# The first loads, the last row tile of layer 1's attention, its thought loop and its gated output of a four-layer Flamingo kernel, put in another order

## The chip, the cores and the metric

The kernel runs on one core of a Trainium2 chip. The metric is the device time of one execution in microseconds (us). The kernel before has 3995.62 us, the median of three runs (3991.7, 3995.62 and 3998.26).

## The reference

A batch of 4 sequences of 512 rows with 512 columns passes four layers. Each layer adds a cross-attention and a feed-forward part, both on layer-normed rows, each scaled by the tanh of a gate:

```
x = x + tanh(g_xattn[i]) * xattn_i(ctx, layernorm(x))      # i = 0, 1, 2, 3
x = x + tanh(g_ffn[i])   * ffn_i(layernorm(x))
```

- Layer 0's attention builds a graph from the context: similarities of projected queries and keys, sigmoid, and of each row only the 153 largest entries are kept. Its feed-forward part is a SwiGLU of width 2048; in this kernel its down weights first pass a Hadamard transform of length 2048.
- Layer 1's attention forms scores of 512 columns for each row, layer-norms them with a gamma and a beta, takes the softmax and adds it to x.
- Layer 1's feed-forward part takes the last row of each sequence, norms it, multiplies it by `agg_w` and repeats four times `thought = thought + (gelu(norm(thought) * pn_gamma + pn_beta) @ d1_w + d1_b) @ d2_w + d2_b` (the gelu is of the product with `d1_w`). Then `broadcast = thought @ bc_w + bc_b`, `gate = sigmoid(x @ gate_w + gate_b)`, and the output is `layernorm(x + gate * broadcast) * out_gamma + out_beta`.
- Layer 2's attention has 32 query heads of 16 columns over 8 key heads. Its feed-forward part is a mixture of 8 experts, top 2.
- Layer 3 is an attention with folded weights and rope, and a SwiGLU.

All data are float32.

## The kernel before

All of x lies in SBUF as `X`, 16 tiles of 128 rows; a batch has four. Each engine has its own program, and the programs are joined by semaphores. A big area `AR` is used by every stage in turn. PSUM has four pairs of banks (BM, BR, BS, BT), each pair a ring.

**The start.** SyncE (SP) issues the loads one after another (L2605 to L2614): the first batch of x, the whole context `CT`, the identity, the gates, gamma; then the query and key weights, the Hadamard matrix and the 4 MB of down weights; then the rest of x, and four writes of zeros to a routing table in DRAM (L2617). PE, ACT and DVE all wait for the first five. DVE norms batch 0 and adds its share of it (`add_norm`). PE and ACT make the similarities. Then DVE and ACT find the 153rd largest entry of each row by a search in 32 steps: in each step both count how many entries lie above a trial value (L728 on DVE, L639 on ACT), and DVE sets the next trial. Beside it POOL does four stages of butterflies of the Hadamard transform, two instructions of 128x4096 each (L307). After the search DVE keeps the top entries (`keep_top`, L766 to L775), PE turns the graph (`turn_graph`), then PE multiplies 16 tiles by the 128x128 Hadamard matrix (L581), and ACT takes each from PSUM (L665). Then comes the transpose of the normed batch (L233), and the loop of layer 0's feed-forward part, in which the other three searches and three of the four batches of layer 1's attention are placed beside the products.

**Layer 1's attention, last batch.** After that loop DVE norms batch 3, PE turns it and makes scores for four row tiles (L572), ACT copies them (L652). DVE takes the moments of all four tiles (`l1_moments`), POOL the reciprocal root, DVE norms them, multiplies by gamma, adds beta (L821), takes the maximum, ACT the exponentials (L657), and DVE adds them to x (`l1_add`). Then SP copies the last row of the batch to a tile of four rows, `XL`, and `l1f_vector` begins.

**The thought loop.** DVE norms `XL` twice; PE multiplies it by `agg_w` (L994); DVE adds a bias (L1184) and norms it (`norm_thought`: moments L1150 to L1152, root on POOL, L1154, times gamma L1155, plus beta L1156, all on 4 rows of 512). Each of four steps: PE turns the four rows (L987), DVE copies them (L1189), PE multiplies by `d1_w` (L1047), DVE adds a bias (L1198), ACT takes the gelu, PE turns and multiplies by `d2_w` (L1064) and sums four parts (L1068), DVE adds a bias (L1212) and the old thought (L1213), and norms. Where DVE waits for PE it does pieces of the norms of x that the gates need (`x_moments`, `x_rows`) and adds beta to x (`add_beta`, L1181). PE does one of batch 0's four gate products per step (L1012). The last `norm_thought` result isn't used.

**The gated output.** PE makes small products of the thought (L1002). Then for batch 1, 2 and 3: two gate products, the transposes of the previous batch's mixed rows (`turn_mixed`, L1020), two gate products, and the norm's transposes of the next batch (L233), which for the last of the three is batch 0, for layer 2's queries. ACT takes the sigmoids (L1091), the copies (L1096) and the norm's scaling (`scale_rows`, L1101); DVE mixes (`mix_gate`, L1227), takes moments (`out_moments`, L1234), and adds to x (`add_mixed`, L1246 and L1248). The order is written out by hand in each engine's program. DVE cuts the queries in two parts (L1269), SP stores them (L1488) and loads them spread out over heads (L1473).

**Layer 2.** PE, ACT, DVE and POOL all wait until x is done for layer 1 (`x_done` of 4 * B); SP waits for its third batch. PE makes the scores of the first two head groups (L1546), DVE their maxima (L1726), POOL cuts the maxima in two parts (`cut_max`), PE turns them (L1555), ACT copies them, SP puts them into the query tile, and the loop of layer 2 begins. In it, batch by batch, the routing of tokens to experts is worked out, and POOL scatters each token's number to its slot in the table, 128 numbers of 4 bytes per DMA, 8 DMAs per batch (`scatter_tokens`, L1409). For the last batch this is done in `moe_pool`; when all have landed, POOL gathers rows of the table (L2135), PE turns them, and the expert loop starts.

Of the kernel before, what the change touches and what calls it, by code (L numbers as in the profile page):

```python
# [13 lines left out]
P = 128  # L14
# [12 lines left out]
TW = NT + 2  # L27
EK = 3
# [62 lines left out]
def flamingo(nc, x, ctx_n, ctx_t, gates, gamma_raw, ident, l0_wq, l0_wk, hadamard, l0_w13, l0_w2, l1_wk, l1_bk, l1_bk_row,  # L91
# [3 lines left out]
    with ctx:  # L95
# [159 lines left out]
        WH = [a(HID // P, D), a(HID // P, D)]  # L255
        TRIAL_I, DROP_I, DROP_P = TRIAL.bitcast(I32), DROP.bitcast(I32), BS[:, 0, 0:ST].bitcast(I32)
# [11 lines left out]
        COLS = a(2 * KT)  # L268
        OROWS = a(2, D)
        BCT, T0 = a(4 * B), a(4 * B)  # L270
        assert a.here() <= FFN_AREA, a.here()
# [13 lines left out]
        def keys_pool(pool):  # L285

            pool.wait_ge(l0f.m.full, 2 + ST + HAD_M)
            nc.gpsimd.tensor_copy(KXH.bitcast(F32R), CT).then_inc(kx_hi, 1)
# [6 lines left out]
        def had_pool(pool):  # L295

            pool.wait_ge(l0_had, 32)
            n = 0
            for stage in range(4):
                w = 1 << stage  # L300
                of, to = WH[stage % 2], WH[1 - stage % 2]
# [140 lines left out]
        HAD_M = HID // P  # L442
        NU = B * ST * UG
# [3 lines left out]
        FFN0_DONE = 3 * B - 1  # L447

# [50 lines left out]
        def l0_tensor(pe):  # L499
# [69 lines left out]
            def l1_scores():  # L569
                pe.wait_ge(f.m.free, m.now() + 2)  # L570
                for st in range(ST):
# [3 lines left out]
            pe.wait_ge(l0_w, 32)  # L575
# [7 lines left out]
            norm_tensor(pe)  # L583
            pe.wait_ge(turn.free, T_PE.now() + 2)
            for b in range(B):
                for g in range(ST):
# [16 lines left out]
                    if g == 2 and b:  # L603
                        l1_scores()
# [11 lines left out]
            l1_scores()  # L616

        def l0_scalar(act):
# [8 lines left out]
            def similarities(b):  # L627
                act.wait_ge(graph_ready, b * ST + 1)
# [20 lines left out]
            def l1_scores(b):  # L649
                act.wait_ge(prob1_used, b + 1)  # L650
                for st in range(ST):
                    nc.scalar.copy(PROB1[:, st, :], full(act, f.m, m)).then_inc(f.m.free, 1)  # L652

            def l1_exp(b):
                act.wait_ge(norm1_ready, b + 1)
                for st in range(ST):
                    nc.scalar.activation(PROB1[:, st, :], PROB1[:, st, :], ACT.Exp, bias=NEGM1[:, st:st + 1],  # L657
                                         accum_out=SUM1[:, st:st + 1]).then_inc(exp1_done, 1)

            project()  # L660
            similarities(0)
            count(BITS)
            tr.step()
            for t in range(HAD_M):
                nc.scalar.activation(WH[1][:, t, :], full(act, f.m, m), ACT.Copy, scale=float(HID ** -0.5)).then_inc(f.m.free, 1)  # L665
# [37 lines left out]
            l1_exp(B - 1)  # L703

        def l0_vector(v):
# [9 lines left out]
            scale1 = float(512 ** -0.5)  # L715
# [86 lines left out]
            def l1_moments():  # L802
# [8 lines left out]
                nc.vector.tensor_scalar(VAR1, MV[:, :, 1], scale1 * scale1, EPS_INNER, ALU.mult, ALU.add).then_inc(var1_ready, 1)  # L811

            def l1_normed(b):
                v.wait_ge(root1_ready, b + 1)
                link(v, nc.vector.tensor_scalar(RS1, RS1, scale1, None, ALU.mult))
# [35 lines left out]
            v.wait_ge(x_rest, 16)  # L851
# [56 lines left out]
            l1_moments()  # L908
            l1_normed(B - 1)
            l1_max()  # L910
            l1_add(B - 1)

        def l0_pool(pool):

            def root1(b):
                pool.wait_ge(var1_ready, b + 1)
                nc.gpsimd.tensor_tensor(RS1, VAR1, HALF[:, :], ALU.pow).then_inc(root1_ready, 1)

# [12 lines left out]
            root1(B - 1)  # L931
# [4 lines left out]
        COL["bc"], COL["gate"] = COLS[:, 0:KT], COLS[:, KT:2 * KT]  # L936
        a = area(FFN_AREA)
        GT, OT, ON = a(KT, S), a(KT, S), a(ST, D)
# [5 lines left out]
        TB = a(4, D)  # L944
# [1833 lines left out]
```

## Time and profile before

| | |
|---|---|
| median of three runs | 3995.62 us |
| the profiled execution | 4001.03 us |
| its span, first to last instruction | 3999.2 us |
| PE busy | 3661.6 us (92%) |
| DVE busy | 1982.6 us (50%) |
| ACT busy | 1377.6 us (34%) |
| POOL busy | 355.7 us (9%) |
| mean share of DMA engines on the main hardware queue | 21.0% |

The busy row of PE in 40 slices of 100 us is 9 or more nearly everywhere. It is 1 in the first slice (0 to 100 us), 8, 6, 7 and 8 between 800 and 1200 us, and 5 from 1600 to 1700 us. So one looks at these places, and there the waits of PE and the chain of waits tell what PE waits for.

### The profile page before, as it was taken

The page shows a single profiled execution, that of the slowest core. Times are in us where ns is not written, and L with a number is a line of the kernel's source. Part 1 is how long each engine was busy: PE and PEld are TensorE (multiplying, and loading weights), DVE is VectorE, ACT ScalarE, POOL GpSimd, SP SyncE. Part 2 cuts the span into 40 slices and gives each one's busy share as a digit, 9 for nine tenths or more (in the row PEclk, how much of TensorE's full clock was granted, in tenths as well). Part 3 has the DMA queues.
Part 4 walks back from the last instruction along what each step waited for, and adds up shares of the span by engine and source line. Part 5 has one row for each costly group of instructions (what it writes and reads, how often), then busy time and mean ns, then how long its engine had stood idle before and what let it go on. Part 6 is the DMA issues. An engine that isn't in the chain of part 4 may idle for free.

```text
span 3999.2 us, 35714 instructions
## 1 busy us (share of the span) xinstructions
PE 3661.6 (92%) x11789; PEld 1695.6 (42%) x11790; DVE 1982.6 (50%) x3587; ACT 1377.6 (34%) x2838; POOL 355.7 (9%) x380
## 2 busy tenths in 40 slices
PE   1999999986789999599879999999999999999999
PEld 0444444432445444356534444444444434444443
DVE  8556666145678776211156756656565652111111
ACT  5524242011357667122233443434343441100100
POOL 7000000000123231211111100000000000000000
PEclk6999999998889999799989999999999999999999
DMA  3321312300322322455532101010101102222221
GB/s 119 126 79 54 132 57 75 112 23 22 86 69 62 74 59 82 156 162 160 170 133 67 50 32 36 24 36 24 36 24 36 36 1 84 85 78 79 84 84 52
DMA packets 78347, 295.90 MB, mean 74 GB/s; under 512 B 10856, under 2 KB 11752, under 8 KB 66684
## 3 DMA queue, kind: packets, MB, share of 16 engines
q1 hardware_dynamic: 69856, 268.35, 21.0%
q0 software_dynamic: 8352, 25.78, 2.1%
q8 instruction: 77, 1.26, 0.1%
q14 instruction: 62, 0.51, 0.0%
HBM read 255.73 MB, written 33.64 MB: 72 GB/s over the span
## 4 chain that ended last, share of the span: by engine, by line
PE 79%; DVE 8%; issue 7%; ACT 3%; DMA 2%; POOL 1%; SPq 0%; DVEq 0%; POOLq 0%; ACTq 0%
PE BM L2293 6%; PE BM L2348 5%; PE BM L529 5%; PE BR L529 5%; PE BR L2357 4%; PE BM L364 4%; PE BR L364 4%; PE BS L2331 3%; PE BS L545 3%; PE BT L545 3%; PE BT L2340 3%; PE BM L2306 3%; PE BR L1989 3%; PE BM L1978 2%; PE BR L1978 2%
## 5 line engine op out<-in xcount | busy, mean ns | idle before, releaser
L2422 ACT ACTIVATE AR<-BS,AR 128x512 f32<-128x512 f32 x256 | 174.5, 685 | 411.5 <-DVE AR L2517 411.5
L2416 ACT COPY AR<-BM 128x512 f32<-128x512 f32 x340 | 198.8, 585 | 307.2 <-PE BM L2348 99.9
L2530 DVE SCALAR_TENSOR_TENSOR X<-BR,AR,X 128x512 f32<-128x512 f32 x256 | 191.9, 750 | 206.2 <-PE BR L2357 197.1
L2517 DVE TENSOR_REDUCE AR<-BS 128x2 f32<-128x1024 f32 x128 | 156.9, 1226 | 253.8 <-PE BS L2331 253.8
L2357 PE MATMUL BR<-AR 128*128 128x512 f32 x512 | 254.8, 621 | 4.2 <-DVE X L2530 0.6
L2348 PE MATMUL BM<-AR 128*128 128x512 f32 x512 | 246.7, 594 | 0.0
L2293 PE MATMUL BM<-XT,AR 128*128 128x512 f32 x512 | 236.6, 605 | 0.7 <-ACT XT L239 0.7
L364 PE MATMUL BM<-XT,AR 128*128 (+1 forms) x512 | 231.7, 595 | 4.9 <-DMA AR<-l_w_dram 4.9
L419 DVE TENSOR_TENSOR AR<-AR,BR 128x512 f32<-128x512 f32 x64 | 44.0, 688 | 379.5 <-PE BR L364 379.5
L529 PE MATMUL BM<-XT,AR 128*128 128x512 f32 x512 | 230.6, 593 | 0.9 <-ACT AR L632 0.9
L529 PE MATMUL BR<-XT,AR 128*128 128x512 f32 x512 | 230.2, 592 | 0.0
L364 PE MATMUL BR<-XT,AR 128*128 (+1 forms) x512 | 230.2, 592 | 0.0
L1664 ACT ACTIVATE PT<-BS 128x512 f32<-128x512 f32 x340 | 192.4, 596 | 86.1 <-PE BS L1562 81.4
L639 ACT ACTIVATE AR<-AR 128x512 f32<-128x512 f32 x256 | 182.6, 714 | 88.8 <-DVE AR L751 88.6
L728 DVE TENSOR_SCALAR_CACHE_REDUCE AR<-AR 128x512 f32<-128x512 f32 x264 | 186.3, 743 | 3.5
L2340 PEld LDWEIGHTS BT<-ID,AR 128*128 128x128 f32 x1024 | 128.6, 142 | 136.8 <-issue 125.3
L1726 DVE TENSOR_REDUCE NEG<-BM 128x2 f32<-128x1024 f32 x129 | 157.6, 1221 | 53.5 <-PE BM L1546 52.0
L2428 ACT COPY AR<-BT 128x512 f32<-128x512 f32 x256 | 151.5, 592 | 75.0 <-PE BT L2340 74.8
L1726 DVE TENSOR_REDUCE NEG<-BR 128x2 f32<-128x1024 f32 x127 | 155.0, 1221 | 41.1 <-PE BR L1546 38.0
L226 POOL TENSOR_TENSOR RSTD<-VAR,HALF 128x4 f32<-128x4 f32 x32 | 32.6, 1020 | 1550.9 <-DVE VAR L2546 930.3
L399 ACT ACTIVATE AR<-BM 128x512 f32<-128x512 f32 x64 | 38.3, 598 | 362.3 <-PE BM L364 362.1
L1562 PE MATMUL BS<-QS,KS 128*128 128x512 f32 x340 | 149.2, 441 | 14.7 <-DMA QS<-MTS 12.3
(383 smaller groups left out, 5919.0 us busy)
## 6 DMA issues: line engine op xcount, KB each, us to landing
AR<-l_w_dram SPq DMA_DIRECT2D x128, 512.0 KB, 3.5
AR<-l_wq_dram SPq DMA_DIRECT2D x32, 1152.0 KB, 5.2
AR<-l_w_dram SPq DMA_DIRECT2D x42, 768.0 KB, 4.9
AR<-w2h SPq DMA_DIRECT2D x16, 1024.0 KB, 4.8
QS<-qx SPq DMA_DIRECT2D x32, 512.0 KB, 10.0
AR<-l_w_dram SPq DMA_DIRECT2D x16, 1024.0 KB, 4.8
AR<-l_w_dram SPq DMA_DIRECT2D x8, 1408.0 KB
made<-AR SPq DMA_DIRECT2D x40, 256.0 KB, 4.9
```

The source lines that it names most:

```text
L364: last = nc.tensor.matmul(bank.rearrange("p (a n) -> p a n", a=1), w[:, kt, a, :], XT[:, ds(b & 1, 1), kt, :], start=kt == 0, stop=kt == K ...
L529: last = nc.tensor.matmul(bank, w[:, kt, a, :], XT[:, b & 1, kt, :], start=kt == 0, stop=kt == KT - 1)
L545: last = nc.tensor.matmul(S_BANKS[st], f.HIDDEN[:, u, st * P:(st + 1) * P], f.DOWN[:, u, :], start=u == 0, stop=u == UG - 1)
L728: nc.vector.tensor_scalar(DUMP[:, st, :], SIM[:, st, :], bound, None, ALU.is_ge, ALU.add, accum_out=COUNTED[:, st:st + 1]).then_inc(found, 1)
L1664: nc.scalar.activation(PT2[:, tt, h, :], evict(("e", n, tt, h)), ACT.Exp, scale=float(HD ** -0.5)).then_inc(e_free, 1)
L1726: nc.vector.tensor_reduce(NEG2[:, n % 2, u // 2, to:to + 2], unit(("s", n, u))[:, 0:2, :], op=ALU.max, axis=AX.X, negate=True).then_inc(s_ ...
L2293: last = nc.tensor.matmul(bank, WS[:, p % 2, at:at + P], XT[:, b % 2, kt, :], start=kt == 0, stop=kt == KT - 1)
L2340: last = nc.tensor.transpose(BT[:, L3[job] % 2, st * P:(st + 1) * P], PROB3[h][:, st, lt * P:(lt + 1) * P], ID[:, :])
L2348: last = nc.tensor.matmul(BM[:, L3[job] % 2, :], KVN[:, p // 8 * ST + lt, :], PROBT3[:, lt, :], start=lt == 0, stop=lt == ST - 1)
L2357: nc.tensor.matmul(BR[:, L3[job] % 2, :], CC3[h][:, st * P:(st + 1) * P], W3[:, p % 8 * 2 + h, :], start=True, stop=True)\
L2416: nc.scalar.copy(to, BM[:, L3[job] % 2, :]).then_inc(m_free, 1)
L2530: nc.vector.scalar_tensor_tensor(out=xb, in0=BR[:, L3[job] % 2, :], scalar=RS3[:, p % 2, h, st:st + 1], in1=xb, op0=ALU.mult, op1=ALU.add) ...
```

## The change

Parts, in the order of the program:

1. First loads: batch 0's quarter of the context, the two weights and the Hadamard matrix come first; PE starts on these four; x, identity and gates follow, then the down weights, the rest of the context and of x. ACT makes its tanh and sigmoid of the gates after its first copies, and takes batch 0's similarities without waiting for DVE.
2. POOL does three stages of butterflies, from the end of `add_norm` on; the fourth is done by PE, which sums two products per tile. Ten of the 16 tiles are put ahead of the graph's turning, and ACT takes five of them between the last five steps of the search.
3. The table in DRAM is 16 times as wide: each 4-byte slot has 64 bytes for itself. It is zeroed by one DMA of 1 MB in 128-byte pieces; a gathered row has 8 KB for 512 bytes.
4. Layer 1's last batch: the fourth row tile, which holds the last row, is scored, normed and added first. The three others are normed by DVE while PE multiplies by `agg_w`, exponentiated by ACT, and added in the first thought step.
5. Thought's gamma and beta are applied to the turned tile (128 rows of 16), `d2`'s bias is added to the thought beside the `d1_w` product, and the unused last norm is left out. The pieces of the norms of x move by one place.
6. The gated output: one gate product ahead of `turn_mixed(0)`, the norm's transposes directly behind `turn_mixed`, and for the last batch ahead of it, so that the queries are cut and stored earlier; `scale_rows` comes before the last sigmoid; DVE's order changes with it. The memsets of layer 2's tiles are done at the end of the thought loop, and SP's copies of these wait only for batch 0's mixing. The last batch is scaled and added to x by POOL.
7. Layer 2's PE, its first maxima on DVE, and the SP no longer wait for the whole of x; ACT's exponentials and DVE's loop do.

```diff
@@ Hadamard on POOL and PE
-            pool.wait_ge(l0_had, 32)
+            pool.wait_ge(l0_had, 16)
+            pool.wait_ge(vec, ADD_NORM)
-            for stage in range(4):
+            for stage in range(HAD_STAGES):          # HAD_STAGES = 3
...
+            def last_butterfly(t):
+                bank, half = start_job(pe, f.m, m), HAD_M // 2
+                nc.tensor.matmul(bank, HAD, WH[0][:, t % half, :], start=True, stop=False)
+                nc.tensor.matmul(bank, HAD if t < half else NHAD, WH[0][:, t % half + half, :], start=False, stop=True)\
+                  .then_inc(f.m.full, 1)
+            pe.wait_ge(l0_w, 64)
             project(0)
             similarities()
+            pe.wait_ge(butterflies, 2 * HAD_STAGES)
+            for t in range(HAD_EARLY):               # 10
+                last_butterfly(t)
+            pe.wait_ge(loaded, 64)
             turn_graph(0)
-            pe.wait_ge(butterflies, 8)
-            for t in range(HAD_M):
-                nc.tensor.matmul(start_job(pe, f.m, m), HAD, WH[0][:, t, :], start=True, stop=True).then_inc(f.m.full, 1)
+            for t in range(HAD_EARLY, HAD_M):
+                last_butterfly(t)
@@ ACT
-            count(BITS)
+            count(BITS - HAD_BETWEEN)                # HAD_BETWEEN = 5
+            for t in range(HAD_BETWEEN):
+                take_hadamard(t)
+                count(1)
@@ layer 1's last batch on DVE
-            l1_moments()
-            l1_normed(B - 1)
-            l1_max()
-            l1_add(B - 1)
+            l1_last_rows()
+            def l1_last_rows():
+                v.wait_ge(f.m.free, m.step() + 2)
+                stats_tiles1(v, ST - 1, ST)
+                v.wait_ge(root1_ready, B)
+                link(v, nc.vector.tensor_scalar(RS1[:, ST - 1:ST], RS1[:, ST - 1:ST], SCALE1, None, ALU.mult))
+                norm_tiles1(v, ST - 1, ST)
+                v.wait_ge(f.m.free, m.step(3) + 2)
+                stats_tiles1(v, 0, ST - 1)
+                add_tiles1(v, B - 1, ST - 1, ST, (B - 1) * ST + 1)
@@ thought
-                link(v, nc.vector.tensor_scalar(TR[0:B, :], TH[0:B, :], ML[0:B, 0:1], RL[0:B, :], ALU.subtract, ALU.mult))
-                link(v, nc.vector.tensor_tensor(TR[0:B, :], TR[0:B, :], TB["pn_g"], ALU.mult))
-                nc.vector.tensor_tensor(TR[0:B, :], TR[0:B, :], TB["pn_b"], ALU.add).then_inc(th_ready, 1)
+                nc.vector.tensor_scalar(TR[0:B, :], TH[0:B, :], ML[0:B, 0:1], RL[0:B, :], ALU.subtract, ALU.mult).then_inc(th_ready, 1)
+            def take_turned():
+                link(v, nc.vector.tensor_tensor(turned, cols(full(v, lr, r)[:, 0:4 * B]), over_b(COL["pn_g"], KT), ALU.mult))
+                nc.vector.tensor_tensor(turned, turned, over_b(COL["pn_b"], KT), ALU.add).then_inc(lr.free, 1)
+            v.wait_ge(root1_ready, B + 1)
+            norm_tiles1(v, 0, ST - 1)                # beside the agg product
...
-                nc.vector.tensor_copy(turned, cols(full(v, lr, r)[:, 0:4 * B])).then_inc(lr.free, 1)
+                take_turned()
+                link(v, nc.vector.tensor_tensor(TH[0:B, :], TH[0:B, :], TB["d2"], ALU.add))
                 if k == 0:
-                    x_moments(1)
+                    add_tiles1(v, B - 1, 0, ST - 1, B * ST)
...
-                link(v, nc.vector.tensor_tensor(TR[0:B, :], bank[0:B, :], TB["d2"], ALU.add))
-                nc.vector.tensor_tensor(TH[0:B, :], TH[0:B, :], TR[0:B, :], ALU.add).then_inc(lr.free, 1)
+                nc.vector.tensor_tensor(TH[0:B, :], TH[0:B, :], bank[0:B, :], ALU.add).then_inc(lr.free, 1)
-                norm_thought()
+                if k < K_STEPS - 1:
+                    norm_thought()
@@ gates on PE                                     # GATES_FIRST = {1: 1, 2: 2, 3: 2}
             for b in range(1, B):
-                for mt in range(2):
+                for mt in range(GATES_FIRST[b]):
                     gate(b, mt)
+                if b == B - 1:
+                    norm_tensor(pe)
                 turn_mixed(b - 1)
-                for mt in range(2, KT):
+                if b < B - 1:
+                    norm_tensor(pe)
+                for mt in range(GATES_FIRST[b], KT):
                     gate(b, mt)
-                norm_tensor(pe)
@@ gates on DVE
             mix_gate(0)
+            x_moments(3)
             out_moments(0)
+            x_rows(3)
             mix_gate(1)
             add_mixed(0)
-            x_moments(3)
-            x_rows(3)
+            x_moments(0)
             add_beta(3)
             out_moments(1)
+            x_rows(0)
             mix_gate(2)
             add_mixed(1)
-            x_moments(0)
-            x_rows(0)
+            cut_first_queries()
             out_moments(2)
             mix_gate(3)
...
             add_mixed(2)
             out_moments(3)
-            add_mixed(3)
@@ POOL, the last batch
+            pool.wait_ge(on_ready, ST * B)
+            xb = X[:, (B - 1) * ST:B * ST, :]
+            nc.gpsimd.tensor_tensor(ON, ON, OROWS[:, 0:1, :].to_broadcast([P, ST, D]), ALU.mult).then_inc(out_norm, 1)
+            pool.wait_ge(out_norm, B + 1)
+            nc.gpsimd.tensor_tensor(xb, xb, ON, ALU.add).then_inc(x_done, 1)
@@ layer 2
-            pe.wait_ge(x_done, 4 * B)                # PE; DVE and ACT: moved behind the first maxima
-            sp.wait_ge(x_done, 3 * B + 1)
+            sp.wait_ge(mix_done, KT + 1)             # ahead of the copies QS, KS
-                sp.wait_ge(x_done, 4 * B)
+                sp.wait_ge(negm_ready, B)            # ahead of the values
@@ the table                                       # APART = 16
-        table = nc.dram_tensor("table", [P * P, 1], F32, kind="Internal").ap()
+        table = nc.dram_tensor("table", [P * P * APART, 1], F32, kind="Internal").ap()
@@ first loads on SP
+            sp.dma_start(CT[:, 0:S], ctx_t[:, 0:S]).then_inc(l0_w, 16)
+            sp.dma_start(WQ0, l0_wq).then_inc(l0_w, 16)
+            sp.dma_start(WK0, l0_wk).then_inc(l0_w, 16)
+            sp.dma_start(HAD, hadamard).then_inc(l0_w, 16)
             sp.dma_start(X[:, 0:ST, :], x_tiles[:, 0:ST, :]).then_inc(loaded, 16)
-            sp.dma_start(CT, ctx_t).then_inc(loaded, 16)
...
+            sp.dma_start(WH[1], l0_w2).then_inc(l0_had, 16)
+            sp.dma_start(CT[:, S:], ctx_t[:, S:]).then_inc(x_rest, 16)
             sp.dma_start(X[:, ST:, :], x_tiles[:, ST:, :]).then_inc(x_rest, 16)
-            for c in range(4):
-                sp.dma_start(table.rearrange("(p n) o -> p (n o)", p=P)[:, 32 * c:32 * c + 32], ZERO[:, :]).then_inc(table_zero, 16)
+            sp.dma_start(table.rearrange("(p a n) o -> p a (n o)", p=P, n=32),
+                         ZERO[:, :].rearrange("p (o n) -> p o n", o=1).to_broadcast([P, P * APART // 32, 32])).then_inc(table_zero, 16)
```

## Rows read from the trace of the kernel before

**Rows 1.** The page, busy us of each engine (share of the span) and instructions.
```profile
PE 3661.6 (92%) x11789; PEld 1695.6 (42%) x11790; DVE 1982.6 (50%) x3587; ACT 1377.6 (34%) x2838; POOL 355.7 (9%) x380
```

**Rows 2.** Timeline, 0 to 120 us: start, duration, engine, line, [idle before, releaser].
```profile
10.55 2.47 DVE L210 BATCH_NORM_STATS2 STAT<-X 128x6 f32<-128x512 f32 x4 [10.55 <-DMA GC<-gamma_raw_dram]
...
17.50 0.60 ACT L631 ACTIVATE AR<-BM 128x512 f32<-128x512 f32 x1 [2.27 <-DVEq L711]
...
20.68 70.95 POOL L307 TENSOR_TENSOR AR<-AR 128x4096 f32<-128x4096 f32 x8 [5.72 <-DMA AR<-l_w_dram]
...
22.79 0.06 DVE L733 MEMSET AR<- 128x4 f32 x1 [2.31 <-ACT AR L632]
...
85.24 6.41 DVE L766 SCALAR_TENSOR_TENSOR AR<-AR 128x2 f32<-128x2 f32 x1
...
96.59 1.97 PE L520 MATMUL BS<-ID,AR 128*128 128x128 f32 x8 [75.12 <-DVE AR L775]
...
100.06 15.66 PE L581 MATMUL BM<-AR 128*128 128x512 f32 x32
...
115.56 1.04 PE L233 MATMUL BT<-ID,XN 128*128 128x128 f32 x8
...
117.77 4.51 POOL L290 TENSOR_TENSOR AR<-AR 128x2048 fp32r<-128x2048 f32 x1
```

**Rows 3.** Windows: stretch, length, busy by engine (instructions), granted clock, DMA share, GB/s.
```profile
100.00:102.00 2.00, 2.00 (x5) 0.97 (x4) 2.00 (x4) 0.00 (x0) 0.00 (x0) 0.50 0.00 0
102.00:104.00 2.00, 2.00 (x5) 0.77 (x5) 1.74 (x4) 1.27 (x3) 0.00 (x0) 0.94 0.00 0
```

**Rows 4.** DMA issues by line: KB each, median us from issue to landing.
```profile
X<-x_dram SPq DMA_DIRECT2D x1, 3072.0 KB, 23.1
...
table<-ZERO SPq DMA_DIRECT2D x4, 16.0 KB, 8.6
...
CN<-ctx_n_dram SPq DMA_DIRECT2D x1, 0.5 KB, 13.3
```

**Rows 5.** Timeline, 887 to 923 us: last batch of attention, start of thought.
```profile
887.91 1.50 DVE L805 BATCH_NORM_STATS2 STAT<-AR 128x6 f32<-128x512 f32 x2 [12.85 <-ACT AR L652]
...
895.27 4.62 DVE L821 TENSOR_TENSOR AR<-AR 128x2048 f32<-128x2048 f32 x2
...
910.27 0.17 DVE L1138 MEMSET AR<- 128x128 f32 x1 [0.66 <-DMA AR<-X]
...
922.99 0.68 DVE L1184 TENSOR_TENSOR AR<-BR,AR 4x512 f32<-4x512 f32 x1 [6.75 <-PE BR L994]
```

**Rows 6.** Groups of DVE, 909 to 1010 us: count, busy us, mean ns.
```profile
L1155 DVE TENSOR_TENSOR AR<-AR 4x512 f32<-4x512 f32 x5 | 3.4, 681 | 0.2
```

**Rows 7.** Timeline, 1003 to 1127 us: end of thought, gates, start of layer 2.
```profile
1003.33 3.70 PE L1012 MATMUL BM<-XT,AR 128*128 128x512 f32 x8
...
1008.90 0.38 PE L987 MATMUL BR<-ID,AR 4*128 4x4 f32 x4 [1.87 <-DVE AR L1156]
...
1064.56 1.04 PE L1020 MATMUL BS<-ID,AR 128*128 128x128 f32 x8
...
1080.13 1.04 PE L233 MATMUL BT<-ID,XN 128*128 128x128 f32 x8
...
1106.49 1.19 PE L1546 MATMUL BM<-KS,QS 128*128 128x512 f32 x2 [11.39 <-DVEq L1715]
...
1120.83 1.57 POOL L1815 TENSOR_SCALAR VW<-CN,G 128x512 f32<-128x512 f32 x1 [13.03 <-DMA AR<-moe_token_dram]
...
1126.53 1.05 PE L1555 MATMUL BS<-ID,NM 128*8 128x128 f32 x4
```

**Rows 8.** Chain of waits, 1600 to 1665 us: start, us, what.
```profile
1637.01 12.43 DMA table<-AR
...
1654.73 3.31 DMA AR<-xnd,AR
```
**Rows 9.** Window of 2 us in that wait, columns as in rows 3.
```profile
1642.00:1644.00 2.00, 0.00 (x0) 0.00 (x0) 0.00 (x0) 0.00 (x0) 0.00 (x0) 0.50 0.00 0
```

More of the change, by code:

```diff
@@ L27 @@
 TW = NT + 2
+APART = 16
 EK = 3
@@ L447, in flamingo @@
         FFN0_DONE = 3 * B - 1
+        SCALE1 = float(512 ** -0.5)
+        TILES1 = {b: (0, 1, 2, 3) if b < B - 1 else (3, 0, 1, 2) for b in range(B)}
         def l0_table():
@@ L615, in l0_tensor, with exp_tiles1, norm_tiles1, add_tiles1 @@
             l1_context()
-            l1_scores()
+            l1_scores(B - 1)
+        def exp_tiles1(act, lo, hi, ready):
+            act.wait_ge(norm1_ready, ready)
+            for st in range(lo, hi):
+                nc.scalar.activation(PROB1[:, st, :], PROB1[:, st, :], ACT.Exp, bias=NEGM1[:, st:st + 1],
+                                     accum_out=SUM1[:, st:st + 1]).then_inc(exp1_done, 1)
+        def norm_tiles1(v, lo, hi):
+            tiles = PROB1[:, lo:hi, :]
+            for st in range(lo, hi):
+                last = nc.vector.tensor_scalar(PROB1[:, st, :], PROB1[:, st, :], MV[:, st, 0:1], RS1[:, st:st + 1], ALU.subtract, ALU.mult)
+            link(v, last)
+            for row, op in ((0, ALU.mult), (1, ALU.add)):
+                link(v, nc.vector.tensor_tensor(tiles, tiles, ROWS1[:, row:row + 1, :].to_broadcast([P, hi - lo, S]), op))
+            nc.vector.tensor_reduce(NEGM1[:, lo:hi], tiles, op=ALU.max, axis=AX.X, negate=True).then_inc(norm1_ready, 1)
+        def add_tiles1(v, b, lo, hi, done):
+            v.wait_ge(exp1_done, done)
+            link(v, nc.vector.reciprocal(SUM1[:, lo:hi], SUM1[:, lo:hi]))
+            link(v, nc.vector.tensor_scalar(SUM1[:, lo:hi], SUM1[:, lo:hi], G[:, 1:2], None, ALU.mult))
+            for st in range(lo, hi):
+                last = nc.vector.scalar_tensor_tensor(out=X[:, b * ST + st, :], in0=PROB1[:, st, :], scalar=SUM1[:, st:st + 1],
+                                                      in1=X[:, b * ST + st, :], op0=ALU.mult, op1=ALU.add)
+            last.then_inc(prob1_used, 1)
+        def stats_tiles1(v, lo, hi):
+            for st in range(lo, hi):
+                last = nc.vector.bn_stats(STAT[:, st, :], PROB1[:, st, :])
+            link(v, last)
+            for st in range(lo, hi):
+                last = nc.vector.bn_aggr(MV[:, st, :], STAT[:, st, :])
+            link(v, last)
+            nc.vector.tensor_scalar(VAR1[:, lo:hi], MV[:, lo:hi, 1], SCALE1 * SCALE1, EPS_INNER, ALU.mult, ALU.add).then_inc(var1_ready, 1)
         def l0_scalar(act):
@@ L1116, in l1f_scalar @@
                 act.wait_ge(mix_done, b * KT + 1 if b > 1 else 1)
[L1117 removed]
+                for mt in range(GATES_FIRST[b]):
                     sigmoid(GT, mt)
+                if b == B - 1:
+                    for kt in range(KT):
+                        nc.scalar.copy(QHL[:, 0, kt, :], full(act, turn, T_ACT)).then_inc(q_hi, 1)
                 take_mixed(b - 1)
[L1120 to L1121 removed]
                 if b < B - 1:
                     norm_scalar(act, (b + 1) & 1)
[L1124 to L1127 removed]
+                for mt in range(GATES_FIRST[b], KT):
+                    sigmoid(GT, mt)
+                    if mt == KT - 2:
+                        scale_rows(b - 1)
             take_mixed(B - 1)
```

162 lines of the change are left out of this document (85 added, 77 removed).

## The prediction, made before the changed kernel was run

> **What bounds the kernel now.** I read the page first: PE is busy 92% of the span [rows 1], and the slices in the section on the profile leave three places where it isn't: the first 120 us, 850 to 1130 us, and 1600 to 1700 us. Outside them the change touches nothing, so each microsecond won or lost in one of the three moves everything behind it. Then the timelines of the three.
>
> In the first, the search runs from 22.79 to 85.24: 32 steps in 62.45, 1.95 each. POOL's butterflies run from 20.68 for 70.95, 8.87 each, and end at 91.6; DVE's first small operation after the search takes 6.41 and ends there too, since it waits for POOL. PE turns the graph from 96.59, does the Hadamard tiles from 100.06, and reaches the norm's transposes only when these are over, at 115.56 [rows 2]. In the second there is one chain from DVE to PE and back; PE waits for it. In the third PE waits for a transfer: the last scatter to the table lands 12.43 after its issue begins [rows 8], though in the wait no engine works and the DMA engines move nothing [rows 9].
>
> **Prologue.** Loads: the first five carry 2.1 MB and free DVE at 10.55 [rows 2]. At about 400 GB/s (2.1 MB in the 5 us before), now 1.5 MB lie ahead: about 8.0, so -2.5. ACT's similarities no longer wait for DVE's end (2.27 at 17.50 [rows 2]); they follow PE, whose project starts some 5 us earlier. Both branches, DVE's 7 us of norm and 2.7 of add_norm and ACT's four pairs, meet at about 18. The search starts at 18.2, not 22.79: -4.6.
>
> POOL now starts when add_norm ends, 18.2 too (the down weights land at about 18), and does 6 instructions: 18.2 + 6 x 8.87 = 71.4. ACT has done 27 steps at 18.2 + 27 x 1.95 = 70.9 and then waits for the first Hadamard tile. A tile is now two products, four matmul pieces. At the half clock a piece takes 0.86 (15.66 / 32 is 0.49 over both levels); the clock stood at 0.50 until 102 and at 0.94 behind [rows 3], 5.5 us after PE began to work at 96.59 [rows 2]. So tile 0 is full at 71.4 + 3.5 = 74.9, ACT goes on at 75.5 and tile 1 is late by about 1.4 too; from then on a tile takes 4 x 0.43 = 1.72 and hides in the step, which grows by 0.2 (0.6 of copy against 0.4 of idle time). The search ends at about 87.5, 2.3 later than now. But the 6.41 is gone: keep_top takes 4.9 from there (91.7 to 96.6), so the graph is ready at 92.7, 3.9 earlier. PE is then still at tile 9; it turns the graph at 93 to 95.3 and has only 6 tiles left, 6 x 1.72 = 10.3: norm's transposes at 105.5, where DVE's norm is ready (two microseconds before). Against 115.56 that is **-10**. Bounds: if PE stays at the half clock, 16 tiles x 3.44 from 71.4 on put the transposes at about 128, +12; if the first tile didn't hold the search, -13. I take -10, since in rows 3 work of this kind raised the clock.
>
> The table's zeros: 8192 rows of 128 bytes on SP's queue, ahead of the first up weights. They start when the rest of x has landed, at about 29 (5.6 + 23.1 [rows 4]). From below: the four old writes, 128 such rows each, were issued 0.6 apart and the last three landed alike 8.6 behind their issue [rows 4], so at most 0.6 per 128 rows: 64 x 0.6 = 38. From above: the load of 2048 rows of 512 bytes landed in 13.3 [rows 4]: 4 x 13.3 = 53. The weights follow at 67 to 82 + 5, and are needed at 110. Cost 0; cover 23 us.
>
> **Last row tile.** Old axis: ACT's first score tile is there at 887.9, DVE's memset, which waits for the copied row, at 910.27 [rows 5]. New: moments of one tile 1.2, root 1.1, scaling 0.6, gamma and beta 2 x 0.69 and maximum 0.6 (a quarter of the tiles in 4.62 for two [rows 5], with fixed parts): 893.1. The exponential (0.9) hides behind the other three tiles' moments, 2.5. Then 1.2 for the add, 1.9 for the row's copy: 898.8, **-11.5**. The deferred scaling, gamma, beta and maximum of three tiles (1.5 + 2 x 1.73 + 1.7 = 7.0) lie beside the agg product; that chain takes 6.75 [rows 5], so DVE is 0.2 late: -11.3. Exponentials of three tiles (2.7) are over before the first step asks for them; their add (3.3) and the d2 bias (0.7) fit the 5.2 of the d1 product. The gate weights are loaded after this add; they land about 2.5 before the first gate product: a thin cover.
>
> **Thought.** Per norm, gamma and beta go: 2 x 0.68 and gaps = 1.43 [rows 6]; the turned tile gets a second small operation: +0.22. Four norms: -4.84. The bias in the four steps: -0.72 each (the same size of instruction), -2.88. At the fourth step's sum the gain is 11.3 + 3 x 0.72 + 4 x 1.21 = 18.3. The last norm is gone, but PE is in its gate product, 1003.33 + 3.70 = 1007.03 [rows 7]; it turned at 1008.90: 1.8 more. **-20.1** up to the broadcast.
>
> **Gates and layer 2.** Batch 1's PE work is the same in another order, and PE is its bound: 0. In batch 3 the queries' transposes ran at 1080.13; between the two first gate products, which ended at 1064.56, and these lay turn_mixed(2) with a wait for DVE, and two gate products [rows 7]. They now come first: at 1064.6. DVE has x ready (x_rows(0) at about 1056 on this axis) and cuts them by 1069, where the store began at 1085.8: queries are in SBUF by about 1084. Then PE: turn_mixed(2) 3.2, two gate products 6.9: 1077.5. ACT sigmoid, scale_rows, sigmoid: 1078.5. DVE: mixing 1079.3, add_mixed(2) 4.6 (the size of L821 [rows 5]): 1083.9, out_moments(3) 5.8: 1089.7. DVE's first maximum of layer 2 followed 1106.49 by 1.3; it is now at 1089.8: -18.0. Its 16 maxima, 1.14 each, set the pace as before, and PE's turn_max moves from 1126.53 [rows 7] to 1108.5. POOL is beside: ACT's scaling until 1092.7, two instructions of 128x2048 at 4.51 [rows 2]: x done at 101.9 past 1000, that is 6.6 before it is needed. The values, 14.5 after 1089.7, are there at 1104, maxima cut at 1106: 2.3 of cover (before, POOL waited 13.03 for them [rows 7], also hidden). **-18.0**. Bounds: if PE kept its full clock after the thought loop, about 4 more; if the cover of POOL or values is gone, or one wait per batch stays, 10 less.
>
> **Table.** Eight scatters of 128 numbers wrote into 64 KB; neighbours in an expert lie 4 bytes apart, so some 16 writes of a scatter fall into one 64 bytes. The row says that the time is spent behind the last moved byte [rows 8, 9]. If it is these writes waiting for each other, a slot of 64 bytes for each takes it away, and the scatter lands like the gather of rows of x, in 3.31 [rows 8]: -9.1. The gather of 1 MB for 64 KB adds 1 MB / 0.4 = +2.4. Together -6.7; bounds -8 and +2.4. I take -6.7, nearer to what the idle DMA engines suggest.
>
> The Trainium skill, page "DMA: Bandwidth & Descriptors", section "Specifications", says that transfers under 512 bytes are done by read-modify-write. By that rule a 4-byte write stays as dear in a wide table, and this part would be +2.4; the trace has no scatter with other spacing to decide it. This is the second rival.
>
> **Sum.** -10 - 20.1 - 18.0 - 6.7 = -54.8. The profiled execution took 4001.03; 4001 - 55 = 3946. It lies 5.4 above the median, so 3995.6 - 54.8 = 3941.
>
> **Rivals.**
> 1. The search is held more than I count, or the gates' new order leaves one wait per batch. For it: ACT has 0.4 idle per step only, and PE must warm up; both are places where I chained three engines. Prologue -4, gates -12: 3941 + 12 = 3953.
> 2. The wide table doesn't shorten the landing and costs its gather: 3941 + 9 = 3950. For it: the elements are still 4 bytes. Against: nothing moves in those 11 us.
> 3. Slower: the zeros. If a row of 128 bytes costs one of the 16 DMA engines more than (110 - 29 - 5) / 512 = 0.15, the first unit of layer 0 waits, and from 0.15 + 55 / 512 = 0.26 on all the gain is lost; at 0.3, 29 + 154 + 5 = 188 in place of 110: +78 - 55, 4018. Against it: 13.3 / 128 = 0.10 for rows of 512 bytes.
> 4. PE doesn't warm between the evictions: +22, 3963.
>
> **Chances.** The sum 0.5, rival 1 0.2, rival 2 0.2, rival 4 0.06, rival 3 0.03, a reordering that gains nothing 0.01. 0.2% is 8 us, what a measurement here tells from no change. Faster 0.95, same 0.02, slower 0.03. The range takes in the clock's 4, the search's 3 and the table's 1.3 below, and as much again for small gains left at 0, and rivals 1, 2 and 4 above: 3926 to 3963.
>
> **What would show it.** Search from about 18 to 87 with one gap of 4 to 5 in ACT at about 71 (Hadamard tile 0); DVE's operation behind the search at 0.2, not 6.4; first transposes at 105. The row's copy 11.5 earlier; thought's steps 18.5 apart, not 20.4; the queries' store 36 earlier in all behind the prologue; layer 2's turn_max 38 + 10 earlier; POOL's last scatter landing in about 4. Wrong would be: PE at 0.50 through the tiles, up weights landing after 105, DVE waiting in the first step for exponentials, PE waiting for the gate weights.

## The result, and the profile after

Before 3994.9 us, after 3922.7 us, medians of 4 runs each: ratio 0.982, 95% interval 0.9803 to 0.9837. The change takes 72.2 off; 54.8 was forecast, and 3922.7 lies 3.3 below the range's lower end. The profiled execution of after took 3922.4 with a span of 3920.6, that of before 4001.0 with 3999.2, so the two traces differ by 78.6. Some 6 of these are the high execution of before.

The page of after, busy us by engine, beside [rows 1]:

```profile
PE 3659.5 (93%) x11821; PEld 1693.0 (43%) x11822; DVE 1960.4 (50%) x3582; ACT 1376.8 (35%) x2839; POOL 348.5 (9%) x380
```

PE's busy time is 2 us shorter and the span 79: what went was waiting. The timeline of after, 0 to 120 us, against [rows 2]:

```profile
10.38 2.47 DVE L211 BATCH_NORM_STATS2 STAT<-X 128x6 f32<-128x512 f32 x4 [10.38 <-DMA GC<-gamma_raw_dram]
...
20.25 0.06 DVE L792 MEMSET AR<- 128x4 f32 x1
...
20.44 53.25 POOL L312 TENSOR_TENSOR AR<-AR 128x4096 f32<-128x4096 f32 x6 [5.67 <-DVE X L780]
...
73.74 2.07 PE L585 MATMUL BM<-AR 128*128 128x512 f32 x2 [58.23 <-POOL AR L312]
...
77.56 0.60 ACT L710 ACTIVATE AR<-BM 128x512 f32<-128x512 f32 x1 [5.14 <-PE BM L586]
...
79.59 0.16 DVE L803 TENSOR_SCALAR BS<-AR 128x2 int32<-128x2 f32 x1 [5.25 <-ACT AR L691]
...
88.04 0.16 DVE L825 SCALAR_TENSOR_TENSOR AR<-AR 128x2 f32<-128x2 f32 x1
...
93.32 1.04 PE L528 MATMUL BS<-ID,AR 128*128 128x128 f32 x8
...
105.47 1.09 PE L234 MATMUL BT<-ID,XN 128*128 128x128 f32 x8
```

The reader sees the forecast's picture: one gap of 5.14 in ACT, the 6.41 of DVE's small operation gone (0.16), the norm's transposes at 105.47 in place of 115.56. POOL starts when DVE's `add_norm` (L780) ends, at 20.44, and is done at 73.69.

Timeline, 876 to 902 us, against [rows 5]: one score tile goes ahead alone and frees the row's copy.

```profile
876.66 0.69 DVE L662 BATCH_NORM_STATS2 STAT<-AR 128x6 f32<-128x512 f32 x1 [10.71 <-ACT AR L704]
...
884.80 0.50 SPq L1042 DMA_DIRECT2D AR<-X  x1
...
886.60 0.17 DVE L1215 MEMSET AR<- 128x128 f32 x1 [1.17 <-DMA AR<-X]
...
899.46 0.67 DVE L1266 TENSOR_TENSOR AR<-BR,AR 4x512 f32<-4x512 f32 x1
```

Timeline, 951 to 1061 us, against [rows 7]: thought's last sum, the queries' transposes, the first product and maximum of layer 2, POOL's two instructions for the last gated batch.

```profile
969.64 0.68 DVE L1299 TENSOR_TENSOR AR<-AR,BR 4x512 f32<-4x512 f32 x1 [1.20 <-PE BR L1140]
...
973.16 0.41 PE L1060 MATMUL BR<-ID,AR 4*128 4x4 f32 x4
...
1024.67 1.04 PE L234 MATMUL BT<-ID,XN 128*128 128x128 f32 x8
...
1050.19 1.19 PE L1640 MATMUL BM<-KS,QS 128*128 128x512 f32 x2 [4.25 <-DMA QS<-qx]
...
1051.42 1.23 DVE L1820 TENSOR_REDUCE NEG<-BM 128x2 f32<-128x1024 f32 x1 [2.01 <-PE BM L1640]
...
1052.45 3.81 POOL L1396 TENSOR_TENSOR AR<-AR 128x2048 f32<-128x2048 f32 x1 [3.23 <-ACT AR L1176]
```

The chain of waits around the table, against [rows 8]. The scatter no longer stands in it as a transfer; the gather behind it, 1 MB now, holds its place:

```profile
1565.70 1.04 POOL table L1505
1566.74 1.20 issue
...
1568.70 0.99 POOL AR L2230
1569.69 5.65 issue
...
1575.57 3.18 DMA AR<-xnd,AR
```

And the part that the prediction did not have: layer 2's loop over heads. The waits of PE in it, summed (us in total, times, longest), first before, 1128 to 1613:

```profile
PE BS L1562 <- DMA QS<-MTS: 12.3, 3, 5.6
...
PE BT L1562 <- DMA QS<-MTS: 1.0, 1, 1.0
```

then after, 1071 to 1543:

```profile
PE BS L1656 <- DMA QS<-MTS: 3.3, 1, 3.3
```

MTS are the turned maxima, which SP writes as rows into the queries' tile, 8 KB at a time. The 3.3 that is left in after is also in before, as a wait of 3.37 at 1130.95, long before the first scatter of the loop (1346.59). The longest wait of before comes after POOL has issued four scatters, from 1346.59 to 1351.53. SP issues two rows between 1352.14 and 1353.33, and PE goes on with them only at 1363.32; the second line is the window of 13 us from the end of this wait, with the granted clock as the third number from the end (1.00 is full speed, 2.4 GHz; 0.50 is 1.2 GHz):

```profile
1363.32 0.80 PE L1562 MATMUL BS<-QS,KS 128*128 128x512 f32 x1 [5.63 <-DMA QS<-MTS]
```
```profile
1363.00:1376.00 13.00, 12.68 (x57) 6.62 (x58) 7.80 (x9) 7.31 (x14) 1.45 (x3) 0.78 0.02 3
```

In after the same two rows are issued between 1295.50 and 1296.69, PE's product at the same place starts at 1300.90 without a wait, and the clock is 1.00 in the 13 us from 1293 on and in the next:

```profile
1306.00:1319.00 13.00, 12.73 (x69) 6.76 (x72) 12.26 (x19) 9.51 (x18) 6.17 (x8) 1.00 0.56 126
```

From the first store of cut queries to the last store of normed rows this loop took 1085.8 to 1612.9 before (527.1) and 1029.5 to 1542.0 after (512.5).

Where the 78.6 of the traces come from, by equal points in both:

| stretch | forecast | traces |
|---|---|---|
| start to layer 1's last norm (861) | -10 | -9.1 |
| context products before the last scores | 0 | -2.1 |
| last row tile, up to thought's first norm | -11.3 | -12.3 |
| thought, up to the broadcast | -8.8 | -12.2 |
| gates, up to the first maximum | -18.0 | -20.7 |
| layer 2's loop | 0 | -14.5 |
| table and routing | -6.7 | -7.7 |
| sum | -54.8 | -78.6 |

### The profile page after: what moved, and what is told of

It is laid out like the page before. It is cut to its first block, busy times and chain, and to the rows that moved or that the text cites. A ratio compares the mean times of both kernels' runs of the same rounds, so it can differ in the third digit from the quotient of the medians.

```text
span 3920.6 us, 35772 instructions
## 1 busy us (share of the span) xinstructions
PE 3659.5 (93%) x11821; PEld 1693.0 (43%) x11822; DVE 1960.4 (50%) x3582; ACT 1376.8 (35%) x2839; POOL 348.5 (9%) x380
## 4 chain that ended last, share of the span: by engine, by line
PE 82%; DVE 7%; issue 6%; POOL 2%; DMA 2%; ACT 1%; SPq 0%; DVEq 0%; POOLq 0%; ACTq 0%
PE BM L2388 6%; PE BM L2443 5%; PE BM L537 5%; PE BR L537 5%; PE BR L2452 4%; PE BM L369 4%; PE BR L369 4%; PE BS L2426 4%; PE BS L553 3%; PE BT L553 3%; PE BT L2435 3%; PE BR L2084 3%; PE BM L2401 3%; PE BT L1666 3%; PE BM L2073 2%
## 5 line engine op out<-in xcount | busy, mean ns | idle before, releaser
L2452 PEld LDWEIGHTS BR<-AR 128*128 128x128 f32 x512 | 86.3, 189 | 171.1 <-DVE X L2625 89.0
```

Source lines behind the costliest of these rows:

```text
L2452: nc.tensor.matmul(BR[:, L3[job] % 2, :], CC3[h][:, st * P:(st + 1) * P], W3[:, p % 8 * 2 + h, :], start=True, stop=True)\
```

## The experiments

All times are medians; 3 rounds each, 5 in the last group. The kernel before stood at 3995.0, 3995.7, 3997.2 and 3994.8 beside the four groups.

**Slots 4 bytes apart in the changed kernel.**

```diff
-APART = 16
+APART = 1
...
-SHIFTED, idx, 15, None, ALU.arith_shift_right
+SHIFTED, idx, 11, None, ALU.arith_shift_right
```

> The changed kernel with table slots 4 bytes apart again, in 64 KB; all else is left as changed. Theory A (in layer 2's loop the rows of maxima, which PE waits for, are held up behind scatters that write neighbouring 4-byte slots): the loop from its first turned maxima to the store of the last normed batch takes 484 to 485 again in place of 470.3, PE waits some 9 us more for the maxima's transfers, and the last scatter lands 12 late: 3922.7 + 7.8 + 14.5 = 3945, 3940 to 3947. Theory B (the loop's 14.5 came from elsewhere: another alignment of the transfers or of the granted clock after earlier parts moved): only the table's own 7.8 comes back, 3930.5, and the loop stays at 470.

3940.8, 18.1 above the changed kernel. The loop takes 523.7 (1029.9 to 1553.6); counted as in the expectation, from the first rows of maxima, it is 481.7 against 470.2 in after, so 11.5 of the 14.5 are back. PE's waits in it and the landing of the last scatter are back too:

```profile
PE BS L1656 <- DMA QS<-MTS: 9.9, 3, 4.3
```
```profile
1577.28 12.15 DMA table<-AR
```

Theory A. Of the 18.1, 7.2 is the table's own chain (last store of rows to the first store of expert rows 58.6, against 51.4); the loop gives the rest, 11.2 in this trace.

**The wide table alone in the kernel before.** The edit is the table's part of the change, nothing else.

```diff
+APART = 16
...
-table = nc.dram_tensor("table", [P * P, 1], ...)
+table = nc.dram_tensor("table", [P * P * APART, 1], ...)
...
-nc.vector.tensor_copy(idx[...], POS)
+nc.vector.tensor_scalar(idx[...], POS, float(APART), None, ALU.mult)
```

> The kernel before with nothing but the wide table (64 bytes a slot) and its zeros, its number arithmetic and its gather. Theory A: 3994.9 - 7.8 - 14.5 = 3973, 3970 to 3976; the loop from its first turned maxima to the last normed batch's store takes 470 and not 484.7, and runs of it agree within 2 us where those of the kernel before spread over 6.6. Theory B (loop gained by alignment): 3987. The zeros cost nothing in either: first up weights still land before 110.

3979.1 (3974.7 to 3980.8), 15.8 below before. The loop takes 512.6 (1083.1 to 1595.7), 470.2 by the expectation's count and as expected; PE waits 3.3 for maxima in it; the last scatter lands in 2.20. The expected 3973 was taken from one high profile of before, and is 6 low; the runs spread as widely as before, so the stalls are not what spreads them. Theory A for the cause; its size in medians is 16 to 18, table and loop together, by this run and the one above.

**Narrow slots, all scatters behind the loop.** (`APART` is 1 and the shift 11 here too.)

```diff
 if routed_batch(n, 6) is not None:
-    scatter_tokens(pool, routed_batch(n, 6), 0)
+    pass
...
-for j in range(2):
-    scatter_tokens(pool, B - 1, j)
+for b in range(B):
+    for j in range(2):
+        scatter_tokens(pool, b, j)
```

> The changed kernel with slots 4 bytes apart and the scatters of batches 0 to 2 taken out of layer 2's loop and issued in front of the last batch's, after the loop. Theory A: without scatters in it the loop takes 470 although the table is narrow; behind it POOL issues 24 more scatters at 1.27 = 30.5 and the last lands 10 late or more: 3922.7 + 30.5 + 7.8 = 3961, up to 3980 if the scatters queue on each other. Theory B: the loop's time doesn't follow the scatters; the end is the same.

3959.5, next to the 3961 of theory A. With a narrow table and no scatter in it, the loop takes 511.9 (1029.5 to 1541.4), and PE waits 3.3 for maxima. Behind it 32 scatters queue on each other:

```profile
1579.60 33.11 DMA table<-AR
```

From the first issue at 1540.0 to this landing at 1612.7 it is 72.7 for 32, 2.27 each, against the 1.27 that POOL takes to issue one. So the stalls come with dense scatters inside the loop, and with nothing else that was varied. That a row of maxima lands late because it has to pass such scatters on its way is the reading that fits; the traces show PE's wait for the row and not what held the row up.

**How far apart is far enough.** Only APART and the shift differ from the changed kernel (`APART` 4 and a shift of 13, then 2 and 12).

> The changed kernel with slots 16 bytes apart in place of 64: the table is 256 KB, its zeros a quarter, its gather 256 KB and not 1 MB. Theory A1 (a write is held up only by neighbours in the same 64 bytes, so the cost grows with how many share one): four share one instead of sixteen, the last scatter lands in 2.3 + 10.2 x 3/15 = 4.3, gather 1.8 shorter, loop nearly free of stalls: 3923, 3920 to 3927. Theory A2 (any write closer than some larger distance is held up alike, as with a rule on transfers under 512 bytes): the landing stays at 12 and the loop at 484: 3943. Theory A3 (16 bytes already suffice): 3921.

> The changed kernel with slots 8 bytes apart, a table of 128 KB. Slots 16 and 64 bytes apart let the last scatter land in 2.2, 4 bytes apart in 12.15. If what counts is how many bytes of a small unit (16 or 8) two writes share: 8 bytes may be as free as 16, landing 2.2, gather 0.3 shorter than at 16: 3917.5. If the unit is 16 bytes: two slots share one, a landing of some 5 and stalls of 2 to 5 in layer 2's loop: 3922 to 3926.

> The changed kernel with slots 16 bytes apart once more, beside the changed kernel itself on the same chip: 3917.9 again, 4 to 5 below it; from the traces 2.3 of it is the shorter gather (3.35 in place of 5.65 behind its issue). If the rest was the granted clock of the prologue and not the table, it lies between 2.3 and 5 here.

> The changed kernel itself, as the other side of the comparison: 3922.7, 3921 to 3925.

16 bytes: 3917.9, and 3919.0 in the second group; 8 bytes: 3918.8; the changed kernel beside them 3921.6. The last scatter lands, at 16 and at 8 bytes:

```profile
1564.38 2.23 DMA table<-AR
```
```profile
1565.49 2.38 DMA table<-AR
```

A3, and no A1: there is no slope with the number of slots in 64 bytes. Slots of 8 bytes are as free as those of 64. The gain over 64 bytes is the smaller gather, 3.35 behind its issue at 16 bytes and 3.16 at 8, in place of 5.65; the medians of one chip differ by 2.7 and 2.8, whose ranges overlap (3915.9 to 3923.5, 3917.3 to 3921.8, and 3919.4 to 3923.0). Either is the best version here by a little.

**Dense slots, neighbours far apart.** `APART` is 1 and the shift 11 again; the order is changed only where the table is written, so this kernel leaves out reading the tokens back from where they were put.

```diff
-tensor_scalar(idx[...], POS, float(APART), None, ALU.mult)
+tensor_scalar(idx[:, part], POS, float(APART), None, ALU.mult)
+tensor_scalar(LOW[:, part], idx[:, part], P - 1, 7, ALU.bitwise_and, ALU.logical_shift_left)
+scalar_tensor_tensor(out=at[:, part], in0=idx[:, part], scalar=7, in1=LOW[:, part],
+                     op0=ALU.logical_shift_right, op1=ALU.bitwise_or)
...
-ap=(IDX0, IDX1)[j][:, tile:tile + 1]
+ap=(AT0, AT1)[j][:, tile:tile + 1]
```

> The changed kernel with slots 4 bytes apart in 64 KB, but slot s of tile t at place 128 s + t: two slots that follow each other in a tile lie 512 bytes apart, and what lies in the same 8 bytes is written by scatters of other batches or not at all. Two more small DVE operations per number row (some 0.2 each). The tokens read back are others than those that were routed, so the experts work on other rows of x, as many; this part of the computation is changed. Theory P (writes of one scatter that share 8 bytes hold each other up): the last scatter lands in 2.2 to 2.5 and PE's wait for maxima stays at 3.3 in all; 3921 + 1 = 3922. Theory Q (a table of 4-byte slots in 64 KB is slow in whatever order it is written): 12 and 10, 3941.

3921.1, PE's wait for maxima 3.3 in all. Behind the last scatter the chain goes on without waiting for a landing:

```profile
1568.18 0.96 POOL table L1510
...
1571.10 0.99 POOL AR L2235
```

Theory P. The table is as small and its slots as narrow as before; only what one scatter writes side by side has changed. So it is neither the size of the write nor that of the table. The total hides two things: the gather of 64 KB is 2.65 shorter than that of 1 MB (3.00 behind its issue and not 5.65), and the loop takes 515.8 (1028.4 to 1544.2), 3.3 longer than in after. Of this, 1.6 is PE's waits for DVE's maxima (9.3 and not 7.7), and DVE has the two added operations per number row; the rest stays open.

**Thought's chain made longer.**

```diff
 v.wait_ge(root_out, root.step())
+for _ in range(2):
+    link(v, nc.vector.tensor_tensor(TR[0:B, :], TH[0:B, :], TB["d2"], ALU.add))
 nc.vector.tensor_scalar(TR[0:B, :], TH[0:B, :], ML[0:B, 0:1], RL[0:B, :], ALU.subtract, ALU.mult)
```

> The changed kernel with two more row operations (4x512, 0.68 each, 1.43 with gaps) on the chain of each of the four norms of thought; their result is overwritten. Theory C (the steps shrank by more than the operations taken out because PE's granted clock no longer falls between its bursts of products): with 1.43 more per norm PE's pauses are nearly as long as before, its clock falls again and the first product of a step (d1, 32 matmuls) takes 5.3 and not 3.64; the four norms cost 4 x 1.43 + up to 5: 3922.7 + 8 to 11 = 3932. Theory D (the clock follows something else, not the pauses): 3922.7 + 5.7 = 3928.4 and products of 3.64.

3932.7, 10.0 for 5.7 of operations. The first product of the second and third steps, after and then with the padding:

```profile
922.15 3.64 PE L1119 MATMUL BR<-AR 128*32 128x512 f32 x32 [0.57 <-DVE AR L1235]
...
938.92 3.64 PE L1119 MATMUL BR<-AR 128*32 128x512 f32 x32 [0.56 <-DVE AR L1235]
```
```profile
926.90 5.34 PE L1119 MATMUL BR<-AR 128*32 128x512 f32 x32 [0.57 <-DVE AR L1237]
...
947.07 5.34 PE L1119 MATMUL BR<-AR 128*32 128x512 f32 x32 [0.56 <-DVE AR L1237]
```

Theory C in the main. In the traces the first step's two products take 6.54 and 5.21 (5.34 and 3.64 in after) and the first product of the next two 5.34; but in the fourth step, behind the same pause of 1.31 as in the second and third, it takes 3.64, and the second product 3.64 where after has 5.31. That sums to 4.5 beside the 5.7. So a longer pause goes with a lower clock in three of four steps, and by itself it doesn't settle it. Windows of 20 us show the granted clock (the column behind the engines), after and then padded:

```profile
917.00:937.00 20.00, 17.15 (x99) 6.67 (x97) 11.07 (x21) 2.28 (x4) 1.03 (x2) 1.00 0.00 1
```
```profile
917.00:937.00 20.00, 15.90 (x98) 5.88 (x94) 10.51 (x19) 2.28 (x4) 1.36 (x2) 0.91 0.00 1
```

**The butterflies undone.** Four stages, one product a tile, nothing between the search's steps; the new loads stay. (Not shown: the two buffers of the butterflies change places, and PE's wait for them moves behind the graph.)

```diff
-HAD_STAGES, HAD_EARLY, HAD_BETWEEN, ADD_NORM = 3, 10, 5, 2 + ST
+HAD_STAGES, HAD_EARLY, HAD_BETWEEN, ADD_NORM = 4, 0, 0, 2 + ST
...
-nc.tensor.matmul(bank, HAD, WH[0][:, t % half, :], start=True, stop=False)
-nc.tensor.matmul(bank, HAD if t < half else NHAD, WH[0][:, t % half + half, :], start=False, stop=True)
+nc.tensor.matmul(bank, HAD, WH[0][:, t, :], start=True, stop=True)
```

> The changed kernel with four stages of butterflies on POOL and one product for each Hadamard tile, all behind the turned graph, as before the change; the first loads stay in their new order. If the split alone made the prologue's gain: search 20.3 to 82.7, POOL done at 91.4, DVE's first small operation behind the search takes about 8, tiles from 100, the folded down weights stored at 116 and not at 106.2: 3922.7 + 9.8 = 3932.5. If the new order of loads and the end of the search's hold matter too, it is 4 to 5: 3927.

3929.8, between the two forecasts. The small operation waits again, and the folded weights are stored at 115.68:

```profile
83.25 8.73 DVE L822 SCALAR_TENSOR_TENSOR AR<-AR 128x2 f32<-128x2 f32 x1
```

So the split made nearly all of the prologue's gain (9.5 of 10.2 at that store), the loads by themselves next to nothing: a search that starts earlier only waits longer for POOL. At 861 us 8.5 of the 9.5 is left, in medians 7.1.

**The last gated batch back on DVE.**

```diff
 add_mixed(2)
 out_moments(3)
+add_mixed(3)
```

(with POOL's two instructions taken out).

> The changed kernel with the last batch's scaling and addition of the gated rows back on DVE, ahead of layer 2's maxima. If POOL's instruction was what moved the maxima forward: two operations of 128x2048 at 2.3 lie on the path again, 3922.7 + 4.6 = 3927.3. The rival is that the maxima then wait for the queries' and keys' rows from memory anyway: 3922.7 to 3924.

3928.3, so 5.6 above. POOL's instructions were what moved the maxima. On DVE stand two operations of 2.29 and a wait of 2.99 of the first of them for ACT's scaling, which the forecast left out; the idle time before the first maximum is 1.53 and not 2.01. That sums to 7.1; the trace has the first maximum at 1057.99 and not 1051.42, 6.6 later. Why 5.6 in medians is a little less stays open.

**Small loads ahead of x.**

```diff
-sp.dma_start(X[:, 0:ST, :], ...).then_inc(loaded, 16)
-sp.dma_start(ID[:, :], ident).then_inc(loaded, 16)
 sp.dma_start(G[:, :], ...).then_inc(loaded, 16)
 sp.dma_start(GC[:, 0:1], ...).then_inc(loaded, 16)
+sp.dma_start(X[:, 0:ST, :], ...).then_inc(loaded, 16)
+sp.dma_start(ID[:, :], ident).then_inc(x_rest, 16)
...
```

> The changed kernel with the two small rows of gates loaded ahead of x and the identity behind it, counted by themselves. In the changed kernel x landed at 8.0 but DVE waited until 10.38 for the gate row queued behind it. If the queue's order is the cause: DVE starts at 9.0, search and POOL's butterflies 1.4 earlier, and since PE's tiles follow POOL the prologue ends 1.4 earlier: 3921.3. If the loads are bound by their start-up and not by the order: no change, 3922.7.

3921.9 (3918.2 to 3924.6): no change that can be told. DVE's start:

```profile
10.26 2.47 DVE L211 BATCH_NORM_STATS2 STAT<-X 128x6 f32<-128x512 f32 x4 [10.26 <-DMA X<-x_dram]
```

x now lands last, in 6.6 and not 5.4. The order within the queue is not what holds the start: DVE gains 0.12, and the first Hadamard tile goes out 0.25 earlier.

## Why the prediction was right in sign and short in size

The step that failed is the first paragraph's "Outside them the change touches nothing". The table's part was priced only at the end, in the wait for the last scatter. But 24 of its 32 scatters are issued inside layer 2's loop, three times eight, and SP's rows of maxima are issued among them. Before, PE waited for such a row behind the scatters of a batch (5.6 and 1.0, then 3.3), and then ran its next products at a lower granted clock (0.78 in the 13 us behind the longest of these waits, 1.00 at the same place of after). The scatters were on no critical chain there, so I did not look at what they delayed. That is a wait put at nothing. The runs put table and loop together at 15.8 (alone) to 18.1 (undone), where the term was 6.7: 9 to 11 of the 17.4 that the forecast is short. The rest is spread over the steps below; their differences are read from the two traces, of which that of before is some 6 high.

The range hid a slip besides: 3941 less 8.3 and "as much again" is 3924.4, not 3926. The result lies under that too.

By its steps:

- **Loads.** x landed at 8.0 as worked out, but the wait counts the gate rows too, which landed at 10.2: 0.17 and not 2.5. This step failed, and it was passed on: POOL starts behind `add_norm`, at 20.44 and not 18.2, so its butterflies ended at 73.69 and not 71.4.
- **Search and Hadamard tiles.** The first tile went out at 77.56 (75.5 forecast), 2.1 late because POOL was; PE's first two pairs of pieces took 2.07 and 1.91, at a granted clock of 0.50 (1.2 GHz) until 78, about as forecast. Then 1.5 was won back, since the second tile was ready when ACT had counted and was not 1.4 late: the search ended at 88.0 (87.5) and the transposes ran at 105.47 (105.5). That -10 came out is in part luck, two misses of opposite sign. PE did warm up between the evictions, at 78.6: rival 4 is out. 1.3 was then given back in the first unit of layer 0, where PE's clock stood at 0.66 to 0.77 from 121 to 127; the run with the butterflies undone shows the same from the other side, 1.0.
- **Zeros.** 1 MB of them held nothing. They had landed at 36.1 (issued at 7.1, 29.0 to landing), where 67 to 82 was forecast: that is 5.9 behind the rest of x, and the 38 to 53 put on them was far too high. Rival 3 is out.
- **Last row tile.** From the first tile's moments to the memset 9.9, forecast 10.9. The 2.1 in front of it (eight context products in 3.71 and not 5.84) is the granted clock and not the change: the kernel before with the wide table alone has it too (its row copy lies 37.8 behind the first load of the thought's rows, not 39.9).
- **Thought.** The operations are those counted (7.0 at the fourth sum). 3.4 more came from the clock: the first product of a step took 3.64 in three of four steps and not 5.34, one second product 5.31. The prediction had a bound for the clock in the gates and none here; the padded run, with 1.43 us more a step, loses 4.5 to the clock.
- **Gates and layer 2.** -20.7 against -18.0, within the bound given for a full clock: it was 1.00 from 997 to 1037, and the last two gate products, which took 8.80 in before, take 7.03. The new limit is one that was not foreseen: the first product waits for the queries' rows until 1050.19, as DVE comes free.
- **Table.** The landing fell from 12.43 to 2.20, as the run with the wide table alone shows it (forecast 3.3), and the gather grew by 2.4 (3.29 to 5.65 behind its issue), as worked out. Rival 2 is out. The rule of the Trainium skill behind it, page "DMA: Bandwidth & Descriptors", section "Specifications", that writes under 512 bytes are read-modify-write, may hold, but it is not what cost the time: with slots 8, 16 or 64 bytes apart 4-byte writes land in 2.2 to 2.4, and with dense slots in the far order the chain doesn't wait for them.

My mechanism for the table ("writes waiting for each other") fits the runs, its unit was wrong: 8 bytes shared are enough to be slow and 64 shared are harmless. That a write to such a pair waits for the other one is inferred; the runs show only that dense neighbours in one scatter are slow, and at which spacing they are not. Nor do they tell whether it is the shared 8 bytes or that the two writes touch: slots of 4 bytes do both, slots of 8 bytes neither.

## What to carry to other kernels

When a transfer is found slow on the critical chain, look for every other place where the same instruction is issued, and at what shares its queues or engines there: its price may be paid by someone else. Scattered 4-byte numbers should not share 8 bytes with others of the same scatter; a stride of 2, or an order that keeps neighbours apart, is as good as a stride of 16 (3918.8 and 3921.1 against 3921.6) and cheaper to read back. In a chain of short bursts on PE, 1.43 us of pause more or less in a step went with another clock of the next burst in three of four steps here, so state a bound for that in every such chain.

## What the runs showed of the hardware

- A scatter of 128 numbers to dense 4-byte slots took 2.27 where many queued, and the last of eight landed in 12.15 to 12.43; with slots of 8, 16 or 64 bytes in 2.20 to 2.38. In the wait the DMA engines are shown moving nothing [rows 9].
- Transfers of 8 KB that SP issued among them were late: PE waited 5.6, 3.3 and 1.0 for these in the loop of before, and not at all at these places once the slots were apart or the scatters outside the loop.
- Zeros for 1 MB in one transfer landed 29.0 behind their issue; each of the four transfers of 16 KB took 8.3 to 22.2 (estimate from their issues at 6.1 to 21.2: all landed some 24 behind the first issue). Both were issued behind the load of the rest of x, which landed at 28.7 and 30.2.
- With the same products and 1.43 us more on DVE in each step of the thought loop, PE's first product of 32 matmuls took 5.34 and not 3.64 in the second and third step, and 3.64 as before in the fourth; the granted clock of the 20 us around the second was 0.91 and not 1.00.
